# Adapter product, base layer and LoRA on one core: the block products take their matmuls grouped by kind

## The reference

```python
y        = jnp.einsum('bsi,boi->bso', x, weight[adapter_ids])
base_out = jnp.einsum('btd,od->bto', y, base_W) + base_b
logits   = jnp.einsum('btd,nd->btn', y, router_W) + router_b
probs    = softmax(logits); w = top-8 probabilities summed by expert (expert_map)
h        = jnp.einsum('btd,erd->bter', y, A)
lora     = jnp.einsum('bter,eor->bto', h * w[..., None], B) * 2.0
out      = x + base_out + lora
```

## Time and profile before

| what | value |
|---|---|
| time, median of 3 runs | 402.16 us (400.67 to 402.24) |
| the profiled execution | 401.29 us |
| its span, first to last instruction | 399.5 us |
| granted TensorE clock, mean | 0.999 |
| PE busy | 394.5 us (99%), 2102 matmuls |
| PEld busy (weight loads, beside PE) | 348.5 us (87%), 2102 loads |
| DVE, ACT busy | 301.1 us (75%), 158.6 us (40%) |
| DMA | 67.56 MB, mean 169 GB/s |

### The profile page before, as it was taken

The page is one execution under the profiler, slowest core; times in us unless marked ns, Lnnn a source line. Parts: engine busy times, 40 slices in busy tenths (PEclk is TensorE's granted clock), DMA queues, the critical chain, the costliest instruction groups (busy, mean ns, idle before and its releaser), DMA issues.

```text
span 399.5 us, 5973 instructions
## 1 busy us (share of the span) xinstructions
PE 394.5 (99%) x2102; PEld 348.5 (87%) x2102; DVE 301.1 (75%) x554; ACT 158.6 (40%) x226; POOL 8.5 (2%) x22
## 2 busy tenths in 40 slices
PE   8999999999999999999999999999999999999996
PEld 7889888898888988889888888888888898888985
DVE  2867998798968984789657996589846798467763
ACT  3766444672156402554026620355304542144300
POOL 0002210000000000000000000000000000000000
PEclk9999999999999999999999999999999999999999
DMA  7999598830457305652076510775026830464002
GB/s 290 401 391 400 97 203 270 295 108 0 174 194 263 105 0 210 208 219 99 0 263 223 200 50 24 260 277 174 0 86 230 308 110 0 147 222 158 2 0 105
DMA packets 27133, 67.56 MB, mean 169 GB/s; under 512 B 3442, under 2 KB 14194, under 8 KB 26994
## 3 DMA queue, kind: packets, MB, share of 16 engines
q1 hardware_dynamic: 25106, 62.47, 44.3%
q0 software_dynamic: 1872, 3.90, 4.9%
q10 hardware_dynamic: 144, 1.05, 0.7%
HBM read 58.08 MB, written 8.39 MB: 166 GB/s over the span
## 4 chain that ended last, share of the span: by engine, by line
PE 97%; DMA 1%; SPq 0%; DVE 0%; issue 0%
PE y_ps L825 29%; PE y_ps L827 15%; PE pl_ps L849 7%; PE x_ps L863 6%; PE x_ps L864 6%; PE x_ps L862 6%; PE s_ps L863 6%; PE s_ps L862 6%; PE s_ps L864 6%; PE pl_ps L852 4%; PE s_ps L877 1%; PE s_ps L879 1%; PE s_ps L878 1%; DMA w_raw<-in_wT 1%; PE y_ps L838 1%; PE x_ps L879 0%
## 5 line engine op out<-in xcount | busy, mean ns | idle before, releaser
L825 PE MATMUL y_ps<-x_split,w_hi 128*128 128x512 f32 x504 | 176.0, 393 | 0.0
L827 PE MATMUL y_ps<-x_split,w_lo 128*128 128x256 f32 x504 | 141.3, 280 | 0.0
L825 PEld LDWEIGHTS y_ps<-x_split,w_hi 128*128 128x128 f32 x504 | 94.4, 187 | 21.7 <-issue 0.4
L827 PEld LDWEIGHTS y_ps<-x_split,w_lo 128*128 128x128 f32 x504 | 95.4, 189 | 0.3
L395 ACT CAST w_hi<-w_raw 128x1024 fp32r<-128x1024 f32 x58 | 60.8, 1050 | 77.3 <-DMA w_raw<-in_wT 77.2
L521 DVE TENSOR_TENSOR w_lo<-w_raw,w_hi 128x1024 fp32r<-128x1024 f32 x58 | 70.9, 1224 | 16.4 <-ACT w_hi L395 14.8
L387 ACT COPY y_sum<-y_ps 128x256 f32<-128x256 f32 x63 | 23.4, 372 | 56.8 <-PE y_ps L827 56.8
L539 DVE TENSOR_TENSOR y_sum<-y_ps,y_sum 128x256 f32<-128x256 f32 x63 | 26.4, 419 | 18.5 <-ACT y_sum L387 18.1
L849 PE MATMUL pl_ps<-pl_split,y_hi 128*128 128x480 f32 x128 | 33.0, 379 | 0.0
L862 PE MATMUL s_ps<-st_hi,y_hi 128*128 128x464 f32 x80 | 30.4, 380 | 0.0
L863 PE MATMUL s_ps<-st_lo,y_hi 128*128 128x464 f32 x80 | 29.9, 373 | 0.0
(11 more groups left out here) (114 smaller groups left out, 538.4 us busy)
## 6 DMA issues: line engine op xcount, KB each, us to landing
w_raw<-in_wT SPq DMA_DIRECT2D x60, 512.0 KB, 3.7
res<-in_x SPq DMA_DIRECT2D x16, 512.0 KB, 5.0
x_raw<-in_xT SPq DMA_DIRECT2D x14, 512.0 KB, 4.9
out<-res SPq DMA_DIRECT2D x13, 512.0 KB, 2.8
early_raw<-in_wT SPq DMA_DIRECT2D x4, 512.0 KB, 8.6
hi_raw<-in_base_t SPq DMA_DIRECT2D x2, 928.0 KB, 9.8
st_raw<-in_base_t SPq DMA_DIRECT2D x2, 928.0 KB, 11.4
st_raw<-in_base_t POOLq DMA_DIRECT2D x2, 928.0 KB, 9.6
```

What stands on the lines that cost most here:

```text
L825: nc.tensor.matmul(y_ps[:, c % 2, :], w_hi[:, s, k, :], x_split[:, k, :, :].rearrange("p s t -> p (s t)"), start=(k == 0), stop=False)
L827: mm = nc.tensor.matmul(y_ps[:, c % 2, 0:T], w_lo[:, s, k, :], x_split[:, k, 0, :], start=False, stop=(k == KC - 1))
```

## The change

Inside `product` the one loop over j, with three matmuls in each round, becomes three loops with one matmul each. The 12 matmuls are the same, with the same operands and the same destination; their order is another. Before, the order is (L862, L863, L864) four times. Now it is four of high y with high base, four of high y with low base, four of low y with high base.

```diff
                 for j in range(KH):
                     nc.tensor.matmul(dst, hi(j), st_hi[:, j, block_of, :], start=begins and j == 0, stop=False, skip_group_check=not begins)
+                for j in range(KH):
                     nc.tensor.matmul(dst, hi(j), st_lo[:, j, block_of, :], start=False, stop=False, skip_group_check=not begins)
+                for j in range(KH):
                     mm = nc.tensor.matmul(dst, lo(j), st_hi[:, j, block_of, :], start=False, stop=(j == KH - 1),
                                           skip_group_check=not begins)
                 return mm
```

## The result

The changed kernel takes 403.24 us (median of 8 runs, 402.74 to 404.15), the kernel before 401.57 us (8 runs, 400.67 to 402.24). The ratio of the mean times is 1.0043, with a 95% interval of 1.0030 to 1.0056. So the time is inside the forecast range, and the ratio inside the 0.5% that I called no change, though the interval reaches beyond it. The interval leaves out 1: about 1.7 us were lost. The profiled execution took 403.10 us at a span of 401.3 us, 1.8 us more than before.

A forecast was written before the change was run, and what follows sets the result against it. The prediction took TensorE's unbroken matmul stream to bound the kernel. All terms of the change came to 0, so the median of 402.16 us stayed, rounded to 402.2 us, with a range of 400.5 to 403.6 us.

The forecast's parts named there:

- no change: Whole kernel: time within 0.5% (2.0 us) of before, about what a measurement can tell from none; chance 0.93.
- Bound: TensorE: one unbroken matmul stream from first adapter chunk to last LoRA term; time is the sum of matmul pitches.
- Price of the new order in a product: Pitch difference of the 684 product matmuls from reordering: taken as 0 us, within -1.1 to +1.1 us.
- three sorts of row: Pitches by kind in a product, a LoRA pair sharing a tile, and already grouped plain products; together -1.1 to +1.1 us.
- The 5 ns: L862 to L863 pitch, 207.5 ns against 212.5; if real, parting 228 pairs with one y tile costs 1.14 us.
- Rival A: Products: neighbours with one y tile are cheap, so parting 228 pairs is slower; 12 ns each gives 404.9 us; chance 0.04.
- Weight loads: Products: every matmul has its own 188 ns load, still covered by the matmul before it, so no saving is lost.
- waits: TensorE: waits stay ahead of each product's first matmul; the later first read of low y gains nothing; 0 us.
- end of a product: Last matmul of a product signals at the same distance from the first, so VectorE's additions start as before; 0 us.
- The sum: Whole kernel: profiled 401.29 us plus 0, or as a median of timed runs 402.16 plus 0, rounded to 402.2 us.

The follow-up runs named there:

- the swapped LoRA term: Kernel before, products unaltered, with the last two matmuls of the last LoRA term of elements 1 to 7 exchanged; 401.11 us, ratio 1.0000.
- the kernel that kept the pairs: Against the kernel before, all products keep the two matmuls of one y tile adjacent; only the low y matmuls move behind them; 403.54 us, ratio 1.0059.
- the second: The changed kernel timed once more without edit, against the kernel before; 403.08 us, ratio 1.0054.
- only T4 by kind: Against the kernel before, only the last product of elements 1 to 7, into x_ps, gets the new grouped order; 403.82 us, ratio 1.0058.

## Why the prediction was right, and which step of it failed

- **Bound.** Right: PE's stream is the time, and in both profiles of the changed kernel it has no wait after the first chunk. In two of the other kernels' profiles there is one of 0.5 or 0.6 us, in element 1. The view of waits can also miss a slip of some 0.1 us, as under the swapped LoRA term.
- **Price of the new order in a product.** Forecast 0 within -1.1 to +1.1 us, measured -0.54. All three sorts of row allow for that, and part of it depends on what stands ahead of the products, as the two values of elements 1 and 2 and of 3 to 7 show. I expected 2.51 to 2.55 us for a product; they are 2.49 to 2.55, apart from the one behind the transposes, which holds an extra gap in both kernels. The 5 ns that I read out of twelve pitches are not there in the medians of all 228 pairs (210 ns against 211.5 and 210): a row of 10 ns steps does not carry them.
- **Rival A (shared tile).** Refuted as a mechanism by the kernel that kept the pairs. The kernel did get slower in total, as A said, but for another reason.
- **Weight loads, waits, end of a product.** Right: 188 ns, 1.7 us of waits, and no wait at the end of a product.
- **The sum.** Here it failed. I added the prices of what the change touches and set everything else to 0. The unchanged stage 1 held +2.46 us, in elements 2 to 7, because the grouped T4 leaves the stream in another state. The bounds of -1.1 to +1.1 were bounds of one term; the pitch of the neighbours downstream was put at nothing without a reason. The kernel before showed already that it moves: its element 1 takes 22.60 us and its element 2 takes 22.19 for the same code. I had looked at the pitch inside the products, and never compared the same stage across elements.

That the time lies in the range is luck as much as forecast. The range had its width from the spread of the runs and the bounds of another term, and the median lies 0.36 us below its upper end. The chance of 0.93 for "no change" was right by the bound of 0.5%, and barely: the first comparison gave 1.0043, the second 1.0054. That nothing would move was wrong.

## What to carry to other kernels

In a kernel bound by one unbroken matmul stream, compare the time of one and the same stage across loop iterations before you call a reordering free. If it takes two values that no wait explains, a reordering ahead of it may switch it (the grouping of T4 did, the swap of two LoRA matmuls did not), and the effect of an edit of a few matmuls is then not the sum of its parts. Before a small gain or loss is put down to an edit, look for it in the stages that the edit did not touch; half the edit, and an unrelated small matmul at the boundary, tell it apart.

## What the runs showed of the hardware that was not expected

- A stream of float32r matmuls of 512 and 256 columns, each with its own weight load, has two steady patterns at the same granted clock (1.00 in both windows of element 3): 346.6 ns a pair, or a cycle of three pairs at 353.3 ns each, 1.9% slower. In elements 2 to 7 it keeps one for all 128 matmuls, unless a matmul is put in between them. In element 0 of the kernel with only T4 by kind it went from fast to slow on the way (chunks of 2.77 us, then 2.82 to 2.83), with no gap between matmuls that would show a wait; one pitch of 122 ns stands where 117 did. Element 0 shows a third cycle in some launches (the first one of the changed kernel among them): 231, 112, 233 and 117 ns, at the speed of the fast pattern.
- Which of them it enters is alike for elements 2 to 7 in each of the 13 profiled executions, and the same in both of the one kernel that was profiled twice. For element 0 it differed between those two (19.50 and 19.87 us).
- One matmul of 32 columns at the boundary costs about 0.12 us (27 ns of its own and 88 to 92 in the next pitch) and can switch the pattern in either direction.
- What in the engine the state consists of stays open: the profile shows starts and modelled ends only. That the rhythm belongs to work of other engines is unlikely: its cycle of three pairs does not divide a chunk of eight, and it runs on across chunks all the same (2.830, 2.831, 2.819 us, over and over). But no run took that work away. A short wait on VectorE can switch the pattern, as in element 1 of the kernel with the swapped LoRA term.
